# Second attention: weight tiles turned by VectorE out of 128-byte pieces, instead of by TensorE

## The reference

```python
q = einsum('bsd,ed->bse', x, Wq).reshape(b, s, 32, 128)     # Wq [4096, 512]
k, v = the same with Wk, Wv                                  # [1024, 512], 8 key heads
q, k = rope(rmsnorm(q) ), rope(rmsnorm(k))
k_all, v_all = concat(512 cached keys/values by page table, own 128)
o = softmax(mask(q k_all^T / sqrt(128))) v_all               # 4 query heads share one key head
out = einsum('bse,de->bsd', o, Wo)                           # Wo [512, 4096]
```

## Time and profile before

| | |
|---|---|
| median of 3 runs | 1545.21 us (1545.05 to 1545.4) |
| the profiled execution, its own time | 1531.98 us |
| its span, first to last instruction | 1530.3 us |
| TensorE busy | 97% |
| VectorE, GpSimd, ScalarE busy | 78%, 58%, 57% |
| granted TensorE clock, mean | 0.992 |
| first step of the second attention, (0, 0), starts at | 313.1 us |
| steps (0, 0) to (6, 7) end at | 1327.65 us |

### The profile page before, as it was taken

How to read it: one execution, slowest core, us unless ns; L and a number is a source line. 1 busy time by engine, 2 the same in 40 slices (tenths; PEclk the granted TensorE clock), 3 DMA queues, 4 the chain that set the end, 5 groups by cost and what they waited for, 6 DMA issues and landing times.

```text
span 1530.3 us, 27044 instructions
## 1 busy us (share of the span) xinstructions
PE 1487.2 (97%) x8816; PEld 1270.3 (83%) x8816; DVE 1200.2 (78%) x2688; ACT 869.9 (57%) x2266; POOL 892.0 (58%) x1241
## 2 busy tenths in 40 slices
PE   6899999989999999999999999999999999999997
PEld 4688888778888888888888888888888888888885
DVE  3788887778888887888888888887888888877765
ACT  2332233356666666666666666666666666666641
POOL 4211442256667676766766676666666776676521
PEclk8999999999999999999999999999999999999999
DMA  8996765222212221222122222212221221311102
GB/s 211 224 197 148 163 138 158 70 86 79 70 58 70 78 73 58 71 72 77 60 72 70 73 73 70 71 58 79 72 72 56 78 73 58 91 56 51 43 26 83
DMA packets 158133, 133.38 MB, mean 87 GB/s; under 512 B 106850, under 2 KB 116450, under 8 KB 157994
## 3 DMA queue, kind: packets, MB, share of 16 engines
q1 hardware_dynamic: 140530, 97.56, 23.9%
q0 software_dynamic: 16464, 33.85, 7.4%
q10 hardware_dynamic: 1000, 0.23, 0.1%
HBM read 107.47 MB, written 7.34 MB: 75 GB/s over the span
## 4 chain that ended last, share of the span: by engine, by line
PE 92%; DVE 3%; ACT 1%; issue 1%; DMA 1%; POOL 1%; ACTq 0%; DVEq 0%; POOLq 0%
PE ps_t L969 15%; PE ps_o L771 11%; PE ps_o L773 10%; PE ps_o L772 10%; PE ps_b L771 5%; PE ps_b L773 5%; PE ps_b L772 5%; PE ps_q L773 4%; PE ps_q L772 4%; PE ps_q L771 4%; PE ps_a L771 3%; PE ps_a L773 3%; PE ps_a L772 3%; PE ps_a L827 2%; PE ps_t L794 2%
## 5 line engine op out<-in xcount | busy, mean ns | idle before, releaser
L1463 ACT ACTIVATE sm<-sm,mn 128x640 f32<-128x640 f32 x256 | 211.4, 826 | 232.8 <-DVE mn L1935 232.8
L1811 DVE TENSOR_TENSOR pT_lo<-ps_t,pT_hi 128x512 fp32r<-128x512 f32 x320 | 220.1, 688 | 113.3 <-ACT pT_hi L1386 113.2
L637 POOL DMA_INDIRECT kraw<-in_L_cond_k_cache_dram,idx_a x200 | 197.8, 989 | 88.9 <-issue 73.7
L1386 ACT ACTIVATE pT_hi<-ps_t 128x512 fp32r<-128x512 f32 x320 | 188.5, 589 | 84.6 <-PE ps_t L969 84.6
L637 POOL DMA_INDIRECT vraw<-in_L_cond_v_cache_dram,idx_a x200 | 199.4, 997 | 59.1 <-issue 58.8
L969 PE MATMUL ps_t<-ident,sm 128*128 128x128 f32 x1280 | 195.5, 275 | 2.8 <-ACT sm L1473 1.5
L969 PEld LDWEIGHTS ps_t<-ident,sm 128*128 128x128 f32 x1280 | 148.0, 140 | 50.7 <-DVE qT_lo L1811 17.9
L669 POOL TENSOR_TENSOR z<-pairs_p,zl 128x128 f32<-128x128 f32 x160 | 59.4, 412 | 173.6 <-DVE pairs_p L1670 173.6
L771 PE MATMUL ps_o<-pT_lo,v_hi 128*128 128x512 f32 x320 | 129.8, 406 | 0.0
L773 PE MATMUL ps_o<-pT_hi,v_hi 128*128 128x512 f32 x320 | 125.5, 392 | 0.0
L772 PE MATMUL ps_o<-pT_hi,v_lo 128*128 128x512 f32 x320 | 124.9, 390 | 0.0
(11 more groups left out here) (260 smaller groups left out, 4316.8 us busy)
## 6 DMA issues: line engine op xcount, KB each, us to landing
fv<-st SPq DMA_DIRECT2D x128, 128.0 KB, 2.3
tab<-tab_scratch SPq DMA_DIRECT2D x64, 256.0 KB, 2.6
wblk<-n_L_attn_weight_qkv_dram SPq DMA_DIRECT2D x24, 384.0 KB, 5.6
wpraw<-_L_attn_weight_proj_dram SPq DMA_DIRECT2D x8, 1024.0 KB, 5.6
mask<-mask_scratch SPq DMA_DIRECT2D x64, 128.0 KB, 2.7
wtile<-in_L_cond_Wq_dram SPq DMA_DIRECT2D x28, 256.0 KB, 3.3
wtile<-in_L_cond_Wo_dram SPq DMA_DIRECT2D x28, 256.0 KB, 2.9
kraw<-in_L_cond_k_cache_dram,idx_a POOLq DMA_INDIRECT x200
```

Of the source, the lines that this page charges most:

```text
L637: pool.indirect_dma_start(raw[:, par, c, :], None, rows_d, bass.IndirectOffsetOnAxis(idx[:, k:k + 1].bitcast(U32), 0)).then_inc(arrived[pa ...
L1386: act.activation(dst, src, ACT.Copy).then_inc(t_hi, 1)
L1463: act.activation(sm[:, h, :], sm[:, h, :], ACT.Exp, bias=mn[:, h:h + 1], scale=-1.0, accum_out=den[:, h:h + 1]).then_inc(e_done, 1)
L1811: dve.tensor_tensor(lo, src, hi.bitcast(F32), ALU.subtract).then_inc(t_lo, 1)
```

## The change

The W groups leave TensorE's list. SyncE loads each weight tile in four transfers of 32 partitions each, in pieces of 32 floats (128 bytes), so that the sixteen 32x32 blocks of the 128x512 tile lie where they belong after turning; VectorE turns every block in its place (`dve.transpose`) from `wtile` into `wa_turn` or `wo_turn`, which are the same memory as `wa_lo` and `wo_lo`. ScalarE then rounds from there into the high tile (`turned_hi`), and the low part is made in place: for the first tile of a step by GpSimd one step later, behind `v_lo`; for the second tile of a step (only n = 6 and 7 have two) by VectorE after `DS`. The tiles are spread anew, 1, 1, 1, 1, 1, 1, 2, 2 per step. The columns of the output layer come out in another order for this, which the strided reads of the last layer's weights undo.

```diff
+        wa_turn = at("wa_turn", [P, 2, NC_, PW], F32, 160)
+        wo_turn = at("wo_turn", [P, 2, HG, HID], F32, 64)
...
-        W_FIRST = {0: 0, 1: 1, 2: 3, 3: 4, 4: 6, 5: 7, 6: 9}
-        W_COUNT = {0: 1, 1: 2, 2: 1, 3: 2, 4: 1, 5: 2, 6: 1, 7: 0}
+        W_FIRST = {0: 0, 1: 1, 2: 2, 3: 3, 4: 4, 5: 5, 6: 6, 7: 8}
+        W_COUNT = {0: 1, 1: 1, 2: 1, 3: 1, 4: 1, 5: 1, 6: 2, 7: 2}
...
-                sp.dma_start(wtile[:, slot, :], src).then_inc(wt_in[slot], 16)
+                if t < 6:
+                    blocks = src.rearrange("(j b) (c i a) -> i b c j a", j=4, c=NC_, i=4)
+                else:
+                    blocks = src.rearrange("(b j) (c i a) -> i b j c a", j=4, c=NC_, i=4)
+                for i in range(4):
+                    sp.dma_start(wtile[32 * i:32 * i + 32, slot, :].rearrange("b (u v a) -> b u v a", u=4, v=4),
+                                 blocks[i]).then_inc(wt_in[slot], 16)
...
+                g_of, n_of = (g, n - 1) if n else (g - 1, N - 1)
+                for t in tiles_of(n_of, g_of == G - 1)[:1] if g_of >= 0 else []:
+                    wait_alone(pool, wt_hi, g_of * TILES_W + t + 1)
+                    pool.tensor_tensor(w_dst(wa_lo, wo_lo, (g_of + 1) % 2, t),
+                                       w_dst(wa_turn, wo_turn, (g_of + 1) % 2, t),
+                                       w_dst(wa_hi, wo_hi, (g_of + 1) % 2, t).bitcast(F32),
+                                       ALU.subtract).then_inc(wt_lo_pool, 1)
...
-                    if name[0] == "W":
-                        t = int(name[1:])
-                        w_tile(*idx(name), t, g * (16 * TILES_W // 2) + 16 * (t // 2 + 1))
...
+            def turned_hi(g, t):
+
+                act.wait_ge(wt_turned, g * TILES_W + t + 1)
+                act.activation(w_dst(wa_hi, wo_hi, (g + 1) % 2, t),
+                               w_dst(wa_turn, wo_turn, (g + 1) % 2, t), ACT.Copy).then_inc(wt_hi, 1)
...
+                def turn(t):
+
+                    dve.wait_ge(wt_in[t % 2], (g * (TILES_W // 2) + t // 2 + 1) * 64)
+                    raw = wtile[:, t % 2, :]
+                    if t < 6:
+                        raw = raw.rearrange("p (c m) -> p c m", c=NC_)
+                    else:
+                        raw = raw.rearrange("p (j c a) -> p c j a", j=4, c=NC_)
+                    dve.transpose(w_dst(wa_turn, wo_turn, (g + 1) % 2, t), raw).then_inc(wt_turned, 1)
...
+                if len(tiles) > 1:
+                    t = tiles[1]
+                    dve.wait_ge(wt_hi, g * TILES_W + t + 1)
+                    dve.tensor_tensor(w_dst(wa_lo, wo_lo, (g + 1) % 2, t), w_dst(wa_turn, wo_turn, (g + 1) % 2, t),
+                                      w_dst(wa_hi, wo_hi, (g + 1) % 2, t).bitcast(F32),
+                                      ALU.subtract).then_inc(wt_lo_dve, 1)
```

More of the change, by code:

```diff
@@ L272, in block_program @@
         wt_in = [sem(f"wt_in{i}") for i in range(2)]
+        wt_turned = sem("wt_turned")
+        wt_hi = sem("wt_hi")
+        wt_lo_pool = sem("wt_lo_pool")
+        wt_lo_dve = sem("wt_lo_dve")
         tab_in = [sem(f"tab_in{i}") for i in range(2)]
@@ L336, in block_program, with tiles_of @@
         waits_alone = sem("waits_alone")
-        W_FIRST = {0: 0, 1: 1, 2: 3, 3: 4, 4: 6, 5: 7, 6: 9}
-        W_COUNT = {0: 1, 1: 2, 2: 1, 3: 2, 4: 1, 5: 2, 6: 1, 7: 0}
+        W_FIRST = {0: 0, 1: 1, 2: 2, 3: 3, 4: 4, 5: 5, 6: 6, 7: 8}
+        W_COUNT = {0: 1, 1: 1, 2: 1, 3: 1, 4: 1, 5: 1, 6: 2, 7: 2}
         PRO = HG + 2
         def groups_of(n, last):
+            w = []
             if last:
                 w = [f"L{i}" for i in range(7) if i // 2 + 1 == n] + [f"Y{i}" for i in range(2) if N - 2 + i == n]
-            else:
-                w = [f"W{W_FIRST[n] + i}" for i in range(W_COUNT[n])] if W_COUNT[n] else []
             nxt = not (last and n == N - 1)
             return w + ["K"] * nxt + ["D0", "D1", "D2"] + ["q"] * nxt + ["D3", "DS"]
+        def tiles_of(n, last):
+            return [W_FIRST[n] + i for i in range(W_COUNT[n])] if W_COUNT[n] and not last else []
         PER_G = sum(len(groups_of(n, False)) for n in range(N))
@@ L970, in transposed @@
                 return mm.then_inc(t_full, 1)
-            def w_tile(idx, bank, t, arrivals):
-                pe.wait_ge(wt_in[t % 2], arrivals)
-                transposed(idx, bank, [(c, wtile[:, t % 2, c * P:(c + 1) * P]) for c in range(NC_)])
             def k_group(idx, bank, g, n):
@@ L1143, in step @@
                     if n == N - 1:
[L1144 removed]
+                        pe.wait_ge(wt_lo_pool, g * N + 6)
                     project_q(n1, wpar1, [0, 1])
@@ L1473, in normalise @@
                     act.activation(sm[:, h, :], sm[:, h, :], ACT.Copy, scale=rd[:, h:h + 1]).then_inc(p_act, 1)
-                w = [m for m in names if m[0] in "WLY"]
+                w = [m for m in names if m[0] in "LY"]
+                tiles = tiles_of(n, last)
                 exponentials(0)
@@ L1487, in step @@
                 group("D0")
+                if tiles:
+                    turned_hi(g, tiles[0])
                 exponentials(2)
@@ L1504, in step @@
                 group("D3")
+                if len(tiles) > 1:
+                    turned_hi(g, tiles[1])
                 if nxt:
@@ L1958, in step @@
                     group(w[1])
+                if tiles:
+                    turn(tiles[0])
                 if not (first and n < 1):
@@ L1962, in step @@
                     group("K")
+                if len(tiles) > 1:
+                    turn(tiles[1])
                 group("D0")
```

31 lines of the change are left out of this document (18 added, 13 removed).

## The result

| | before | changed |
|---|---|---|
| median of the timed runs | 1545.22 us | 1519.42 us (1519.08 to 1522.03, 4 runs) |
| profiled execution, own time | 1531.98 us | 1519.61 us |
| its span | 1530.3 us | 1517.9 us |

The ratio of the medians is 0.9837 (95% interval 0.9825 to 0.9848): 25.8 us faster, where 9.9 was forecast. Yet the two profiled executions differ by only 12.4 us. The document has to explain two things: whether those 12.4 us are the steps that the prediction named, and where the other 13 are.

What follows compares the result with a forecast made beforehand. TensorE, busy 97%, was taken as the bound, with GpSimd's stats_k leaving nothing to spare. Gains of 28.2 us less losses of 18.3 gave 9.9; 1545.2 - 9.9 = 1535.3 us, range 1522 to 1549.

Steps and rivals of the forecast that it cites:

- TensorE loses 70 tiles: Weight tiles leave TensorE at 0.44 us each: 30.8 us gained if nothing else got late.
- GpSimd's subtraction, 1.25 us: Added ahead of stats_k in 56 steps; in 49 steps n > 0 against 1.19 us spare, 2 us lost.
- n = 0: Six steps of groups 1 to 6 without spare GpSimd time become 19.27 us: 7.4 lost, the tiles' 2.6 not gained.
- GpSimd's pauses: Late second key gathers, four steps 13 apart, cost 1.6 us each, 6.4 in all; smaller pauses add 1.2.
- (7,0): This step of 20.11 us already waited for GpSimd and loses another 1.25, to near 21.3 us.
- The last layer: Strided reads in some 20 TensorE products cost 0 to 2 us; taken as 0.
- VectorE, ScalarE, transfers: Turns of 0.63 to 0.72 us, the subtraction behind DS, ScalarE's exchanged copy and the smaller-piece loads cost nothing.
- The sum: Gains of 28.2 us less losses of 18.3 give a net gain of 9.9 us, 1535.3 us.
- All hidden: Rival: all or most of GpSimd's subtraction fits in spare time, 1527.7 or 1514.4 us; chance 0.20 for below 1529.
- GpSimd did not come to set every step: Rival: GpSimd's subtraction above 1.49 us sets every step; slower than before above 1.68 us; chance 0.14.
- A late tile: Rival: a weight tile loaded in 2048 pieces comes too late and VectorE stops at its turn; chance 0.03.
- The port lock: Rival: VectorE's 14 two-input SBUF subtractions hold GpSimd, 14 steps grow by 0.6, 8 us, 1543.5 us; chance 0.12.

Runs made afterwards that it cites:

- f4: f1 without GpSimd's third value gather of a step, its wait counts adapted, so the output is another; 1502.65 us, ratio 0.9793 to the kernel before.
- third occasion: Both kernels unchanged, timed again later on another chip: before 1533.58 us, changed 1518.30 us, ratio 0.9902.
- f1: e2 again, unchanged, on another occasion; 1508.91 us, ratio 0.9838 to the kernel before, no held copy.
- e6: e4 with the tiles spread 2, 1, 2, 1, 2, 1, 1, 0 over n = 0 to 7; 1527.99 us, 32 held copies.
- e7: e2 with SyncE's old wait kept and a second one behind it, so only the table and mask loads move later; 1522.71 us, 34 held copies.
- e2: The changed kernel with every low part taken by VectorE behind DS and none by GpSimd; 1529.61 us, 32 held copies.
- e3: The changed kernel with GpSimd's subtraction kept, tiles two each in n = 0, 1, 2, one each in 3 to 6, none in 7; 1514.36 us.
- e4: e2 with SyncE's table and mask loads moved into the next step; 1507.95 us, no held copy.
- f2: e4 again, unchanged, on another occasion; 1507.54 us, ratio 0.9828 to the kernel before, no held copy.
- e5: e3 with SyncE's table and mask loads moved into the next step; 1509.63 us, no held copy.

## Why the prediction was wrong, point by point

**TensorE loses 70 tiles.** Right. Without a tile on TensorE the regular steps take 17.58 us.

**GpSimd's subtraction, 1.25 us.** Right in its sum, by another way: 1.01 us of later start and 0.17 to 0.26 of a longer third gather, against 1.19 to spare. The forecast 0.04 a step was 0.01 (steps of 17.58 instead of 17.57), so 2 us became 0.5.

**n = 0.** Right: 19.13 us against 19.27 forecast, 6.6 us lost against 7.4.

**GpSimd's pauses.** Right, and the part I trusted least: they came again, in steps (1,4), (3,1), (4,6), (6,3), again 13 steps apart, and each made its step 18.8 to 19.0 us long. What they count is gathers: the paused gathers of before and of the changed kernel are number 115, 219, 323 and 427 of the kernel, 104 apart, which is 13 steps of 8. In f4, with 7 gathers a step, they are number 115, 219, 324 and 429, 14 or 15 steps apart. The first three of f4 from the timeline of GpSimd (the first stands behind `stats_k`, where GpSimd idles in any case):

```profile
559.86 1.02 POOL L650 DMA_INDIRECT vraw<-in_L_cond_v_cache_dram,idx_a  x1 [2.62 <-issue]
...
821.04 1.23 POOL L650 DMA_INDIRECT vraw<-in_L_cond_v_cache_dram,idx_a  x1 [2.04 <-issue]
...
1085.93 1.22 POOL L650 DMA_INDIRECT vraw<-in_L_cond_v_cache_dram,idx_a  x1 [2.05 <-issue]
```

The four steps lost 5.3 us against regular ones, where 6.4 was forecast. The 1.2 us for smaller pauses were not lost.

**(7,0).** 21.9, 21.0 and 20.9 us in three profiles, 21.3 forecast. In the first TensorE waited 2.7 us for `v_lo`, and then ran 3.4 us at half clock (below); in the other two the loss was 0.8 to 0.9 us, not 1.25.

**The last layer.** The prediction allowed 0 to 2 us for its strided reads and took 0. All that follows (7,0) took 1.2 us (third occasion) and 1.5 us (first) more than in the first profile of before, where two executions of the kernel before differ by 0.5. No run separates the reads in it.

**VectorE, ScalarE, transfers.** Right. Turns of 0.70 us in the estimated 0.63 to 0.72, the subtraction of 0.69 behind `DS`, neither waited for; no wait for `wtile`.

**The sum.** The steps (0,0) to (6,7) took 999.6 us instead of 1014.6: 15.0 less, where these terms add to 11.2. In executions without held copies (1531.98 before, 1516.69 on the third occasion) the whole difference is 15.3, as it is between the medians of the third occasion; forecast was 9.9. The losses in the steps were each a little smaller than I took them, 12.4 us in place of 17; the 1.2 to 1.5 us behind (7,0) are the one loss that I had put at nothing.

**The step that failed** is the one sentence "the median of the timed runs lies 13.2 above that execution, and I carry the difference over". I treated it as a constant that both kernels have. It is not one: the changed kernel's own profile lies 0.2 us from its median, and the repeat of before, profiled at 1543.43 us, shows what its long executions hold, 27 copies of ScalarE that start late, 9.3 us. Without that sentence the forecast would have been 1522, against 1519.4. That even this lies near is in part luck of the occasion: the gain to compare is 15.3 us, half as much again as the 9.9 of the sum. The range, too, had no case in which the 13.2 us go away.

**The rivals.** "All hidden" at 1514 to 1527 did not happen: the time lies there, but n = 0 and the pauses cost what the other case said. GpSimd did not come to set every step. A late tile did not occur. **The port lock exists**, which I doubted, but it fell where it costs little. In f1, 49 of VectorE's 70 subtractions with two SBUF inputs meet the start of a key gather. VectorE's and GpSimd's timelines in f1, start of step (1,2):

```profile
489.46 0.68 DVE L2026 TENSOR_TENSOR wa_lo<-wa_turn,wa_hi 128x512 fp32r<-128x512 f32 x1
...
489.51 1.58 POOL L650 DMA_INDIRECT kraw<-in_L_cond_k_cache_dram,idx_a  x1 [0.53 <-issue]
491.40 0.94 POOL L650 DMA_INDIRECT kraw<-in_L_cond_k_cache_dram,idx_a  x1 [0.30 <-issue]
```

and the same gather when it starts ahead of the subtraction (f1, start of step (0,7)):

```profile
435.83 1.08 POOL L650 DMA_INDIRECT kraw<-in_L_cond_k_cache_dram,idx_b  x1 [0.53 <-issue]
```

Started 0.03 us ahead, the gather takes 1.08 (6 times). Of 43 that start behind, 7 (0.03 or 0.04 behind) take 1.08 too; the other 36, 0.04 to 0.38 behind, take 1.60 down to 1.26, and each of them ends 1.63 or 1.64 us after the subtraction's start, so 0.96 after its end. In the changed kernel's profile of the third occasion 7 gathers overlapped, 6 of them 0.03 ahead, so one was longer. The Trainium skill says this (page "SBUF — State Buffer", section "SBUF: two separate sides"): whoever starts first has the shared ports for the whole instruction. The trace agrees in that the end of such a gather is set by the end of the subtraction, 490.14 in the rows above, and not by its own start.

The trace of the kernel before had it too, and I overlooked it. VectorE's sum in the rotation, then GpSimd's third value gather, step (6,3):

```profile
1250.88 0.68 DVE L1832 TENSOR_TENSOR rope_a<-rope_a,rope_b 128x512 f32<-128x512 f32 x1
...
1250.98 1.40 POOL L637 DMA_INDIRECT vraw<-in_L_cond_v_cache_dram,idx_a  x1 [0.30 <-issue]
```

Four gathers that start 0.08 to 0.14 us behind this sum take 1.40 to 1.42 instead of 0.94, and end 0.81 to 0.85 after it. The gather of the earlier trace rows starts 0.52 behind and also ends 0.81 after it; so late it can be lengthened by 0.03 only, and my reading of it could not speak against the rule. The changed kernel's longer third gather is the same: it starts 0.29 to 0.39 into the sum (VectorE, 1163.65 to 1164.33 in step (5,7)) and ends 0.82 after it. Even 49 such overlaps cost little in f1, since GpSimd has over 1 us to spare in those steps: all but n = 0, n = 7 and the paused ones took 17.57.

**What stays open.** What holds the copy. It depends on the occasion (the second, with holds, and the last, with none, were on the same chip), and it does not hang on where SyncE's loads of the tables stand (e6 and e7 had holds with the loads moved, f1 none with them in place). That kernels differ on one occasion (e2 32, e3 3) speaks for something in the step's phase. The end of a hold gives a hint that I did not follow. GpSimd's third value gather, SyncE's load of the mask and ScalarE's held copy in the repeat of before, step (4,3), then step (5,3), both with two tiles:

```profile
966.34 0.94 POOL L637 DMA_INDIRECT vraw<-in_L_cond_v_cache_dram,idx_a  x1 [0.30 <-issue]
967.46 0.43 SPq L483 DMA_DIRECT2D mask<-mask_scratch  x1
968.13 0.38 ACT L1390 ACTIVATE kvown<-ps_o 128x256 f32<-128x256 f32 x1 [1.23 <-PE ps_o L773]
...
1113.12 0.94 POOL L637 DMA_INDIRECT vraw<-in_L_cond_v_cache_dram,idx_a  x1 [0.30 <-issue]
1114.70 0.43 SPq L483 DMA_DIRECT2D mask<-mask_scratch  x1
1114.88 0.38 ACT L1390 ACTIVATE kvown<-ps_o 128x256 f32<-128x256 f32 x1 [0.75 <-PE ps_o L773]
```

In (4,3) the gather stands 0.47 us later in the step than in (5,3), the mask's load at the same place, and the copy starts 0.50 later. It starts 0.82 to 0.85 us behind the gather's end both times, but 0.67 and 0.18 behind the load. So it is in 23 of the 25 held copies of the steps (0,0) to (6,7): 0.75 to 0.85 us behind the end of that gather. The other two start 0.07 behind a gather's end. In e2's steps n = 1 to 5 of groups 1 to 6, with the loads at one place, the copies move with the gathers too, at several distances (0.06, 0.5 to 0.6, 0.8 to 0.9 us). So the end of a hold goes with GpSimd's list and not with SyncE's loads. Whether a gather is the cause is not shown: f1 has the same gathers at the same places and no held copy, and f4, which leaves one out, met no holds to remove. Nor is the time of e6 known on an occasion without holds.

**A better version** than both kernels is e4, which f2 repeats: all low parts on VectorE, the loads a step later, 1507.95 us on the occasion on which the changed kernel took 1518.30 and the kernel before 1533.58. But e2 shows that on another occasion such a kernel can lose 20 us. The tile placement of e5 (1509.6) was not met by such an occasion in its form; e3, its neighbour, had 1.2 us of holds on the same occasion on which e2 had 15.

## What to carry to other kernels

When one profiled execution and the timed median of the same kernel differ by more than the effect that you forecast, find out what the difference is before you add it to the other side: profile the kernel a second time and compare the lengths of repeating steps; here 27 of 64 steps named it. Count an engine's spare time step by step: the mean gap of GpSimd would have promised room for the subtraction, and it was the steps without a gap, n = 0 and every thirteenth, that cost 12 of the 28 us gained. And an experiment that removes a suspect proves nothing without its control on the same occasion.
